# Score products of the first block over 32 rows of keys each, and exponentials by pairs of heads

## What is computed

```
h = _layernorm(x) * (1 + ca) + sa
query = heads(ct_q @ Wu_q_w + Wu_q_b) + heads(_rope(ct_q @ Wq_r_w + Wq_r_b))     # 16 heads of 8 features
key   = heads(ct_kv @ Wu_k_w + Wu_k_b) + heads(_rope(h @ Wk_r_w + Wk_r_b))
attn = softmax(einsum('bhqd,bhkd->bhqk', query, key) / scale)                    # 512 x 512 a head
out  = einsum('bhqk,bhkd->bhqd', attn, value)
x = x + ga * (out @ Wo_w + Wo_b)
```

## Time and profile before

| what | value |
|---|---|
| median of 3 runs | 1813.01 us (1808.38 to 1816.07) |
| the profiled execution's own time | 1816.07 us |
| its span | 1816.1 us |
| busy over the span | PE 94%, DVE 82%, ACT 64%, POOL 70% |
| first block, 60 to 296 us | PE 228.39, DVE 186.95, ACT 147.67, POOL 46.41 us busy of 236 |
| second block, 320 to 1816 us | PE 1410.68 us busy of 1496 |

### The profile page before, as it was taken

One profiled execution on the slowest core, in us unless ns is written; L12 is line 12 of the kernel. 1 busy time (PEld: TensorE's weight loads), 2 busy tenths in 40 slices (PEclk: granted clock), 3 DMA queues, 4 the chain that ended last, 5 costly groups with the idle time before them and its releaser, 6 DMA issues.

```text
span 1816.1 us, 61060 instructions
## 1 busy us (share of the span) xinstructions
PE 1709.6 (94%) x25264; PEld 1194.0 (66%) x25264; DVE 1480.6 (82%) x2503; ACT 1158.8 (64%) x2003; POOL 1268.1 (70%) x1541
## 2 busy tenths in 40 slices
PE   8999998699999999999999999999999999999997
PEld 3555554367766767677666677776776767777765
DVE  5887785698878888888788888887988888889873
ACT  3666566457667666766675667666766676667655
POOL 6212112788788777887877887878878888788762
PEclk9999999899999999999999999999999999999999
DMA  2000010465555555555455555555655555555552
GB/s 80 1 7 1 6 43 18 140 202 194 187 168 197 185 178 168 190 193 196 160 176 187 183 188 182 187 173 177 198 190 185 172 186 196 188 179 187 189 171 81
DMA packets 190784, 276.38 MB, mean 152 GB/s; under 512 B 23278, under 2 KB 87340, under 8 KB 190252
## 3 DMA queue, kind: packets, MB, share of 16 engines
q1 hardware_dynamic: 189004, 270.48, 45.2%
q10 hardware_dynamic: 1504, 2.00, 0.3%
HBM read 72.11 MB, written 52.43 MB: 69 GB/s over the span
## 4 chain that ended last, share of the span: by engine, by line
PE 40%; POOL 23%; DVE 14%; issue 9%; ACT 9%; DMA 2%; SPq 1%; POOLq 0%; DVEq 0%; ACTq 0%
DVE turned L983 6%; POOL u L1420 5%; PE psum L596 4%; PE psum L808 4%; POOL sdiff L1409 4%; PE psum L838 3%; PE psum L797 3%; PE psum L667 3%; PE psum L598 3%; PE psum L597 3%; POOL px L1391 3%; PE psum L690 3%; PE psum L776 3%; POOL qT L1420 3%; PE psum L681 3%
## 5 line engine op out<-in xcount | busy, mean ns | idle before, releaser
L983 DVE SCALAR_TENSOR_TENSOR turned<-psum,vecs,tabs 128x1024 f32<-128x1024 f32 x384 | 487.4, 1270 | 47.7 <-POOL u L1420 26.6
L1188 ACT ACTIVATE sq<-psum 128x512 f32<-128x512 f32 x384 | 230.0, 599 | 132.7 <-PE psum L598 130.0
L1420 POOL TENSOR_TENSOR u<-turned,swapped 128x512 f32<-128x512 f32 x192 | 242.6, 1285 | 55.6 <-DMA swapped<-turned 55.3
L1420 POOL TENSOR_TENSOR qT<-turned,swapped 128x512 f32<-128x512 f32 x192 | 243.1, 1288 | 42.1 <-PE psum L776 34.5
L797 PEld LDWEIGHTS psum<-pxT,v 128*64 128x64 f32 x6144 | 194.7, 138 | 73.4 <-issue 66.3
L1409 POOL TENSOR_TENSOR sdiff<-sdiff,rqs 128x512 f32<-128x512 f32 x192 | 200.2, 1042 | 53.0 <-DVE sdiff L1012 51.3
L797 PE MATMUL psum<-pxT,v 128*64 128x64 f32 x6144 | 221.2, 225 | 4.0 <-DMA pxT<-scratch 3.3
L808 PEld LDWEIGHTS psum<-onT,wo 128*128 128x128 f32 x1536 | 199.7, 192 | 27.2 <-issue 8.4
L1391 POOL TENSOR_TENSOR px<-px,rd 128x512 f32<-128x512 f32 x192 | 201.6, 1050 | 20.3 <-DVE rd L1018 18.2
L808 PE MATMUL psum<-onT,wo 128*128 128x128 f32 x1536 | 205.0, 277 | 5.1 <-DVE rT L1059 3.4
L942 DVE TENSOR_REDUCE peaks<-psum 128x1 f32<-128x512 f32 x256 | 170.0, 687 | 42.5 <-PE psum L667 40.4
(11 more groups left out here) (187 smaller groups left out, 3452.3 us busy)
## 6 DMA issues: line engine op xcount, KB each, us to landing
swapped<-turned SPq DMA_DIRECT2D x384, 256.0 KB, 3.0
scratch<-pt SPq DMA_DIRECT2D x192, 256.0 KB
pxT<-scratch SPq DMA_DIRECT2D x384, 128.0 KB
v<-v SPq DMA_DIRECT2D x192, 192.0 KB
w_raw<-in_wqkv SPq DMA_DIRECT2D x36, 256.0 KB, 3.3
v<-v SPq DMA_DIRECT2D x144, 64.0 KB
wo<-in_wo SPq DMA_DIRECT2D x12, 256.0 KB, 3.5
w_raw<-in_w SPq DMA_DIRECT2D x12, 170.5 KB, 2.8
```

The lines of the kernel that those rows point to most:

```text
L983: engine.scalar_tensor_tensor(out=turned[:, n % NROT, :, :], in0=both, scalar=vec(("ks" if which else "qs", i)), in1=tabs[:, 2 * which:2 * ...
L1188: engine.activation(sq[:, n % NSQ, :], bank(n % 2), ACT.Square).then_inc(s_sq, 1)
L1420: engine.tensor_tensor(u[:, n % GT, :] if which else qT[:, m_, :], turned[:, n % NROT, 0, :], swapped[:, n % NSWAP, :], ALU.add).then_inc( ...
```

## The change

Keys are no longer padded: ScalarE writes the packed keys straight to `k3` of shape [128, NG, T], and the copies on GpSimd, the zero fills and the semaphore `s_k3` are gone. A score product takes only the head's own 32 rows of both operands (`head_rows`). A pair of exps was two tiles c of one head; it is now two neighbouring heads for one tile c, in different rows and in different banks, and the exponential writes two heads of `pT` at a stride. `weighted` of a tile waits for the two exponentials of that tile, not for those of all four heads over both tiles. As `k3` is smaller, the buffers that the second block fills early get space of their own, and the waits for `early_a` go.

```diff
-    "pack": dict(tensor=-6.45, scalar=-6.55, gpsimd=-6.136),
+    "pack": dict(tensor=-6.45, scalar=-6.55),
...
-                for hh in range(AG):
-                    put(place + half + hh / 4, "exps", b, g, half, hh)
+                for c, pair in itertools.product(range(2), range(AG // 2)):
+                    put(place + half + c / 2 + pair / 4, "exps", b, g, half, c, pair)
...
-    k3[0] = sb(sa, "k3_even", [P, NG, AG, T], F32R)
+    k3[0] = sb(sa, "k3_even", [P, NG, T], F32R)
...
+    def head_rows(hh):
+
+        return slice(32 * hh, 32 * hh + 32)
...
                 par, g = b % 2, h // AG
+                rows = head_rows(h % AG)
                 pe.wait_ge(*bank_a.empty("pack", b, 0, g))
-                pe.wait_ge(s_k3, b * NG + g + 1)
+                pe.wait_ge(*bank_a.empty("pack", b, 1, g))
                 pe.wait_ge(*bank_a.free(*step))
-                engine.matmul(bk, q3[par][:, g, t * P:(t + 1) * P], k3[par][:, g, h % AG, :], start=True,
+                engine.matmul(bk, q3[par][rows, g, t * P:(t + 1) * P], k3[par][rows, g, :], start=True,
                               stop=True).then_inc(fills, 1)
...
-                b, g, half, hh = k
-                e = nth_a[step] - 1
+                b, g, half, c, pair = k
+                e, t0 = nth_a[step] - 1, (2 * half + c) * P
                 pe.wait_ge(*bank_a.empty("peaks", b, g))
                 pe.wait_ge(s_exp, e - 1)
-                for c in range(2):
-                    t0 = (2 * half + c) * P
-                    m = engine.matmul(bank(2 * (e % 2) + c), k3[b % 2][:, g, hh, t0:t0 + P], q3m[:, g % 2, :], start=True,
+                for j in range(2):
+                    rows = head_rows(2 * pair + j)
+                    m = engine.matmul(bank(2 * (e % 2) + j), k3[b % 2][rows, g, t0:t0 + P], q3m[rows, g % 2, :], start=True,
                                       stop=True)
...
-                pe.wait_ge(s_exp, nth_a["exps", b, g, half, AG - 1])
+                pe.wait_ge(s_exp, nth_a["exps", b, g, half, c, 1])
...
                 if n:
-                    engine.activation(k_all[:, g % 2, :], bk, ACT.Identity, bias=onesc[:, 0:1]).then_inc(empties, 1)
+                    engine.activation(k3[b % 2][:, g, :], bk, ACT.Identity, bias=onesc[:, 0:1]).then_inc(empties, 1)
...
-                engine.activation(pT[:, half, hh, :, :], psum[:, 2 * (e % 2):2 * (e % 2) + 2, :], ACT.Exp,
+                engine.activation(pT[:, half, 2 * pair:2 * pair + 2, c, :], psum[:, 2 * (e % 2):2 * (e % 2) + 2, :], ACT.Exp,
...
-                for hh in range(AG):
-                    rows = slice(32 * hh, 32 * hh + 32)
-                    m = engine.tensor_copy(k3[b % 2][rows, g, hh, :], k_all[rows, g % 2, :].bitcast(F32))
-                m.then_inc(s_k3, 1)
...
             elif kind == "fill":
-                pool.wait_ge(s_k3, copied)
-                pool.wait_ge(*early_a)
...
             if kind == "early":
-                sp.wait_ge(*early_a)
                 load(*FIRST[0])
```

More of the change, by code:

```diff
@@ L404, in build @@
     sa.close()
[L407 to L418, removed]
     sdiff = sb(ctx, "sdiff", [P, HU, 2 * WIN])
@@ L502, in group, with last_exps @@
         return divmod(k, NG)
+    def head_rows(hh):
+        return slice(32 * hh, 32 * hh + 32)
+    def last_exps(b, g):
+        return nth_a["exps", b, g, 1, 1, 1]
     plan = {engine: order(engine) for engine in ("tensor", "vector", "scalar", "gpsimd", "sync")}
@@ L929, in vector @@
                 bv_all = bv[:, :].rearrange("p (o h d) -> p o h d", o=1, h=AH).broadcast_to([P, TT, AH, AD])
-                dve.wait_ge(s_fill, 12 if b else 6)
+                dve.wait_ge(s_fill, 6 if b else 4)
                 dve.wait_ge(s_weighted, 2 * NG * (b - 1))
@@ L945, in vector @@
                 if b * NG + g >= 2:
-                    dve.wait_ge(s_score, nth_a["exps", *group(b * NG + g - 2), 1, AG - 1])
+                    dve.wait_ge(s_score, last_exps(*group(b * NG + g - 2)))
                 dve.wait_ge(*bank_a.empty("pack", b, 0, g))
@@ L1131, in scalar @@
                 b, n, g = k
[L1132 to L1134 removed]
+                if b >= 2:
                     act.wait_ge(*bank_a.empty("peaks", b - 2, g))
[L1136 removed]
+                    act.wait_ge(s_score, last_exps(b - 2, g))
                 act.wait_ge(*bank_a.full(*step))
                 if n:
[L1139 removed]
+                    engine.activation(k3[b % 2][:, g, :], bk, ACT.Identity, bias=onesc[:, 0:1]).then_inc(empties, 1)
                 else:
@@ L1302, in gpsimd @@
         engine.memset(halves_a[:, :], -0.5).then_inc(s_fill, 1)
-        engine.memset(k3[0][:, 0:2, :, :].bitcast(F32), 0.0).then_inc(s_fill, 1)
         engine.memset(peaks[:, :, :, :], 0.0).then_inc(s_fill, 1)
-        copied = normed = 0
+        normed = 0
         for step in plan["gpsimd"]:
             kind, *k = step
-            if kind == "pack":
-                b, n, g = k
-                if n == 0:
-                    continue
-                pool.wait_ge(s_selg, 1)
-                pool.wait_ge(s_fill, 12 if b else 6 + g)
-                pool.wait_ge(s_rstd, 4 * normed)
-                pool.wait_ge(s_k3, copied)
-                pool.wait_ge(*bank_a.empty(*step))
-                if b >= 2:
-                    pool.wait_ge(s_score, nth_a["exps", b - 2, g, 1, AG - 1])
-                for hh in range(AG):
-                    rows = slice(32 * hh, 32 * hh + 32)
-                    m = engine.tensor_copy(k3[b % 2][rows, g, hh, :], k_all[rows, g % 2, :].bitcast(F32))
-                m.then_inc(s_k3, 1)
-                copied += 1
-                if b == 0:
-                    pool.wait_ge(s_k3, copied)
-                    engine.memset(k3[1][:, g, :, :].bitcast(F32), 0.0).then_inc(s_fill, 1)
-                    if g == NG - 1:
-                        engine.memset(vtok[1][:, :, :, :], 0.0).then_inc(s_fill, 1)
-                        pool.wait_ge(s_fill, 11)
-                        engine.memset(vtok[1][:, :, :, AD:AD + 1], 1.0).then_inc(s_fill, 1)
-            elif kind in ("norm", "norm2"):
+            if kind in ("norm", "norm2"):
                 n = norms_a.index(step)
                 pool.wait_ge(s_fill, 1)
-                pool.wait_ge(s_k3, copied)
                 pool.wait_ge(s_mv, TT * (n + 1))
```

37 lines of the change are left out of this document (20 added, 17 removed).

## The result

| what | before | after |
|---|---|---|
| median | 1812.67 us (1808.38 to 1816.07, 4 runs) | 1850.53 us (1839.39 to 1861.38, 4 runs) |
| profiled execution's own time | 1816.07 us | 1839.39 us |
| mean granted clock of its span | 0.987 | 0.961 |

The account below looks back on a forecast made before the run. TensorE's stream was taken to bound the first block from 60 to 296 us. Terms -13 (PE), -1 (start), -2 (block's end) and +3 (waits) gave -13 us, so 1800 us off the 1813.01 median; range 1784 to 1832.

Parts of the forecast that it names:

- rival E: First block: 1.2 GHz clock for another 10% of 236 us adds 12 to 24 us, giving 1812 to 1824; 5%.
- Overlap by rows in float32r: First block's score products: those in different rows run together, 182 overlaps at 0.227 us, 41 us off.
- Rival B: First block: no overlap by rows in float32r, 1840 us; sign: pair ends 0.235 us apart; 15%.
- A change of shape: TensorE's stream, first block: 0.19 us per tile-shape change, 156 becoming 304, so 28 us on.
- Net on PE: TensorE's stream in the first block: -41 from overlap, +28 from changes of shape, -13 us.
- 2 at the end: End of first block: faster pairs close exponential gaps and weighted starts earlier, -2 us (bounds 0 and -3).
- The waits that take its place: First block: waits for banks that DVE must free come into view, +3 us (bounds 0 and 10).
- rival C: First block: PE gains but a bank or ACT is late instead, 1808 to 1814 us, no change; 17%.
- C's sign: First block: DVE's waits for maxima stay but PE's weight loads wait for DVE over 45 us.
- GpSimd's copies, the pairs, the stride, the early loads: First block: removing copies saves 1 us at the start; strided exponentials and early loads 0 us.
- The second block: After the first block: its 1496 us left as they are, beginning when the first ends.
- Rival D: First block: more gain than counted; half the 28 us of shape changes hidden gives 1786 us; 13%.

Follow-up runs that it names:

- f3: The changed kernel with eight unread full products at each wait where the clock falls, two more before every second maximum of the first two groups; 1821.59 us.
- f2: The kernel before with eight unread full products ahead of the first two packs and each step waiting for the bank of norm2; 1808.79 us.
- after_again: The changed kernel once more, unaltered, on another chip; 1847.8 us, 1.0183 of the kernel before.
- e3: The kernel before with 64 tiny 32-row products ahead of pairs of exps, adding 128 changes of shape; 1838.65 us.
- c1: f3 with VectorE taking each maximum over only half of the 512 keys; 1810.28 us.
- e2: The kernel before with pairs of exps by heads, strided exponential and earlier release of weighted, still all 128 rows and GpSimd copies; 1815.21 us.
- e4: The kernel before with score products over 64 rows of padded keys, exps pairs of heads 0, 2 and 1, 3, maxima in that order; 1817.23 us.
- e1: The kernel before with score products cut to the head's 32 rows, padded keys, copies and one-head pairs kept; 1868.51 us.
- f8: The change's order and release with full products at the waits, first two groups over 128 rows, later ones over 32; 1819.63 us.
- f6: e4 with full products at the waits and the first two groups' score products over all 128 rows; 1807.76 us.

## Why the prediction was wrong, point by point

**The step that failed is rival E's dismissal.** It named the mechanism (clock at 1.2 GHz for more of the stage), but sized it at another 10% of 236 us, 12 to 24 us, with a chance of 5%, since "nothing else in the rows speaks for it, since PE stays full". PE did stay full. It was busy 19.76 and 19.82 of 20 us in two slices with a clock of 0.50, so the busy share of a row was the wrong sign to go by. The rows before showed the falls and I read them as short dips caused by idle time; that their length hangs on what PE runs after them was not asked. The sign that rival E named, PEclk below 0.9 where it had been 0.97, came (0.50, 0.67 and 0.71 in three slices of 20 us).

Measured: 123 us low in the block in place of 20, and an end of the block 27.7 us later, where 13 to 16 us sooner was forecast, a miss of 41 to 44 us. Some 5 to 10 of these are the waits of the next paragraphs; the other 34 to 36 go to the clock. The two traces at full clock say the same: f3's last divide transposes start at 301.68, f2's at 310.60, so without low clock the changed stream is 8.9 us ahead, and 27.7 + 8.9 = 37 us are lost to it. The Trainium skill, TensorE: Matmul & The Clock Gate, Terms, gives the penalty as about the throttled time times the missing share of the clock; by that an estimate is 103 x 0.5 = 51 us. The trace is some 14 us below it, and why isn't shown. Between the changed kernel's two traces it fits: after_again has 147 us low in the block, 24 more, and its last divide transposes start at 352.82, 13.0 us later, for 12 by that rule. The median, at 1850.53 us, missed the 1800 by 50 us, more than the trace of the fastest run accounts for; after_again's traced run, with 1858.05 us, shows where more can go. The Trainium skill, TensorE: Matmul & The Clock Gate, Part 1, says that "the default state is throttled, and activity releases the throttle", to which this case adds that a PE which the profile shows as full can be one that doesn't release it (39.58 of 40 us busy at 0.50).

**Overlap by rows in float32r** was right: six products end within 0.60 us in place of 1.41. Rival B (none) fell, but by the sum of the ends and not by the sign that was named: the two products of a pair end 0.22 us apart, not within 0.02, since the second runs first. A reader who went by that sign would have taken it for B. (A small slip besides: the 0.43 us a round of `weighted` is in no row; two rounds take 0.99 us, less 0.19 for the change of shape that is 0.40 each. What L776 shows stands either way.) **A change of shape** was right: 0.43 us end to end in the trace, 0.176 us each in e3 against 0.19, and the trace has the counted 156 changes before and 304 after.

**Net on PE, -13, and 2 at the end** was right as a count and too large as a time. At one clock (f2 against f3) the stretch from the fifth `weighted` step on gains 6 us. **The waits that take its place**, forecast at 3 us, are the term that was mis-sized: 7.7 us more idle time shows ahead of the products alone, near the upper bound of 10 and so near rival C, and c1 shows 5 to 14 us for a faster DVE. C's sign, weight loads that wait for DVE over 45 us while DVE's own waits stay, came in the changed profile as well (60 to 296 us; 30.8 before):

```profile
PEld psum L673 <- DVE peaks L948: 55.8, 85, 1.7
DVE peaks L948 <- PE psum L673: 46.6, 62, 3.1
```

With 8 to 10 in place of 3, -13 - 2 + 8 to 10 is -5 to -7, which is what f3 has.

**GpSimd's copies, the pairs, the stride, the early loads** at nothing: e2 shows nothing for pairs and stride (0.9997). The first maxima can't be judged, since the start ran at the low clock. **The second block** was left as it is, as forecast: 1497.7 and 1503.4 us in the changed kernel's two traces, 1503.9 before. Rival D's gain was nowhere.

**What stays open.** Which property of these products keeps the clock down (rows loaded, rows streamed, or pairs running at once) isn't told apart beyond the number of rows; e4 changed all of them. Pairs running at once aren't needed, by e1, whose two exps of a pair share their rows and which was low for longer than the changed kernel (156 against 114 us from 20 to 320). f8's spread from 1805 to 1835 us was profiled only in a run with a high clock, so where its low time lay in the others was not seen. Why the fourth fall came earlier, behind waits of half a microsecond, isn't shown either. And f2 and f6 stand 7 us apart in the traced block and 1 us in their medians, f2's trace being its slowest run; whether the overlap with 64 rows is worth anything over the full products alone isn't settled.

## What to carry to other kernels

Before cutting a stream of full products into tiles of few rows, look for the waits at which the granted clock already falls, and ask what the stream behind them will be: here four falls grew from 20 to 123 us, though TensorE's idle time hardly did (19.7 of the 300 us from 20 to 320, against 17.0). A full PE in a busy column says nothing on its clock; read that column beside it in every stretch. If the small shape is wanted, keep the first products after a wait at full size, or put unread full products into the wait, and count what two changes of shape cost around each step of another shape.

## What the runs showed of the hardware that was not expected

After the same wait, the clock stayed at 1.2 GHz over two whole slices of 20 us (0.50 and 0.50, PE busy 39.58 of 40) with products over 32 rows; with 128 rows the slice of the wait had 0.83 and the next two 1.00. Added work made a kernel faster: eight unread full products at each of a few waits took 7 us off the kernel before and about 20 off the changed one. Products of half the rows (64) overlap as well, and keep a clock of 0.92 where 32 rows had 0.74 to 0.81. Products in different rows need not run in the order of the program: in 110 of the changed kernel's 128 pairs the second product's record ends ahead of the first's, mostly by 0.22 us, and in none of the 128 before. The exponential that waits for the second alone still never starts before both have ended (0.04 us after, at the least). The low clock is not a fixed tax: one and the same program (f8) ran from 1805 to 1835 us, with its mean clock from 0.994 to 0.975.
